# A new written-out order of the steps in five engine programs, with the last two turns apart from the loop

## The chip, the cores and the metric

The kernel runs on one core of a Trainium2 chip. The core has a matrix engine (TensorE, PE in the rows), VectorE (DVE), ScalarE (ACT), GpSimd (POOL), SyncE (SP), which here only issues transfers, and sixteen DMA engines. The metric is the time of one execution on the device, in microseconds, as a median over runs.

## The reference

The input x has 32 batches of 512 tokens with 256 features. Two blocks follow each other, each added to its input.

```python
x = x + attention(layernorm(x), ...)
x = x + ffn(layernorm(x), ...)
```

Attention works within a batch. For each token: a charge q = tanh(x W_charge + b), its powers q^0 to q^4; a normalised projection (shell), whose product with omega plus a bias goes through cosine and sine; the outer product of powers and waves, times W_combine, gives 64 features phi. The logits are phi phi^T, times a factor that decays with the distance of two tokens, over a temperature; a causal softmax of them weighs the values, and W_out closes.

```python
phi = tp @ W_combine.T
logits = jnp.einsum('bnd,bmd->bnm', phi, phi) * T / temp
attn = jax.nn.softmax(jnp.where(causal, logits, -jnp.inf), axis=-1)
out = jnp.einsum('bnm,bmd->bnd', attn, V)
```

The second block holds 64 slots. A hidden layer (gelu) routes each token to its best 8 of 64 slots by a softmax of these 8 (alpha). Each slot gathers the tokens weighted by alpha, a GRU cell makes new slots of that, and each token receives alpha times the new slots' values.

## The kernel before

The 32 batches go through as 16 pairs k = 0..15, with the two batches of a pair as d = 0, 1. A step is a small function that issues the instructions of one piece of work of one pair on one engine, and its name says what: `proj(k, d, t)` on TensorE is the projection of token tile t. `build()` has one program for each engine, and the order of the steps in each is written out by hand, as a list of calls. An engine works strictly in the order of its program; the five meet only through semaphores, on which a step waits for what it reads and for a free buffer. So the order of the lists decides who waits.

Each program has a prologue (the first pairs, written out), a loop `for it in range(3, NP - 1)` of 12 turns, and a tail (the last pair). One turn works on five pairs at once: it projects pair p = it + 2, does the softmax of n = it + 1, the hidden layer and the routing of f = it, the slots of m = it - 1, and the additions to the output of g = it - 2. PSUM's eight banks are dealt out in three rings in the order in which steps take them.

The steps that the text names. TensorE: `first_warm` (L588) and `warm(n)` (L593), matmuls whose result nobody reads; `weights_setup` and `bias_setup` (L311), which multiply the weight matrices together; `xn_t` and other transposes (L317); `proj` (L343); `phi` (L388, L390); `logits` (L409 to L415); `e_t`, the transposes of the softmax (L317); `values` (L438); `hidden` (L466); `route` (L478); `rt_t` (transposes of the routing logits) and `al_t` (of alpha) (L317); `gather` (L500); `gi_t`; `gx_rz` and `gx_n`, the gates (L515); `slot_v` (L559); `out_mm` (L579). VectorE: `ln_stats` (L883), `xn_low` (xl, L889), `vs` (L902), `qk_full` (QK, L961 and L962), `row_max` (L971), `attended` (L979, L983) and its `lm_stats` (L994), `xm_low` (xmL, L1002), `top` and `shift` (the choice of 8 slots), `gathered` (rw, GIN, L1053 to L1059), `slot_values` (SV, L1098), `finish` (L1107), and `end_norm_a`, `end_norm_b` (xm of pair 15, d = 0 and 1, L264). ScalarE: `ln_norm` (xn, L708), `sine` (L742), `z_copy` (Z, L750), `expo` (E, L759), `gelu`, `gi_copy` (GI, L811), `rz_tanh`. A function outside the table that ScalarE has at hand makes it load another one first (ACT_TABLE_LOAD). GpSimd: `square`, `power` (L254), `ln_scale`, `lm_scale` and others.

SyncE issues the loads of x (`load_x`, L1488, one 512 KB batch each), of the weights (`weight_loads`: W_shell, omegaT, W_scT, counted on the semaphore wa; `first_loads`: eleven, from log_temp to the second row of decay; `slot_loads`: seventeen), the moves `z_moves`, which bring the powers of Z to the partitions where phi reads them as xmT (L1503), and the stores (L1512, L1516). x has ten buffers. TensorE's `weights_setup` waits for wa.

The order of SyncE's program before, and TensorE's loop and tail:

```python
load_x(0); weight_loads(); load_x(1); load_x(2); first_loads(); load_x(3); slot_loads()
...
hidden(z, 0); hidden(z, 1)
gx_n(y)
warm(4)
route(z); al_t(y); rt_t(z); out_mm(x, 1)
warm(21)
gather(z); slot_v(y); gi_t(z)
```

(x, y, z are pairs 13, 14, 15.)

Of the kernel before, what the change touches and what calls it, by code (L numbers as in the profile page):

```python
# [88 lines left out]
def build(nc, a, out):  # L89
    ctx = ExitStack()  # L90
    with ctx:
# [204 lines left out]
        def _(e):  # L296
# [333 lines left out]
            first_warm()  # L630
            weights_setup(); xn_t(0, 0, 0); xn_t(0, 0, 1); bias_setup(); xn_t(0, 1, 0); xn_t(0, 1, 1)
            proj(0, 0, 0); proj(0, 0, 1); proj(0, 0, 2); proj(0, 0, 3); xn_t(1, 0, 0); xn_t(1, 0, 1)
            proj(0, 1, 0); proj(0, 1, 1); proj(0, 1, 2); proj(0, 1, 3); slot_setup(); gates_setup()
            xn_t(1, 1, 0); q_t(0); proj(1, 0, 0); proj(1, 0, 1); xn_t(1, 1, 1); proj(1, 0, 2); proj(1, 0, 3)
            proj(1, 1, 0); z_t(0); proj(1, 1, 1); phi(0); proj(1, 1, 2); logits(0, 0); proj(1, 1, 3)
# [5 lines left out]
            values(1, 0); e_t(1, 2); xm_t(0, 0, 0); proj(2, 1, 3); e_t(1, 3); values(1, 1); values(1, 2)
            xm_t(0, 0, 1); values(1, 3); xn_t(3, 0, 1); logits(1, 2); xm_t(0, 1, 0); xm_t(0, 1, 1)
            e_t(1, 4); hidden(0, 0); hidden(0, 1); e_t(1, 5); e_t(1, 6); values(1, 4); q_t(2); route(0)
            xn_t(3, 1, 0); values(1, 5); z_t(2); xn_t(3, 1, 1); rt_t(0); values(1, 6); e_t(1, 7)
            proj(3, 0, 0); values(1, 7); proj(3, 0, 1); proj(3, 0, 2); phi(2); xn_t(4, 0, 0); proj(3, 0, 3)
            proj(3, 1, 0); xm_t(1, 0, 0); logits(2, 0); proj(3, 1, 1); proj(3, 1, 2); e_t(2, 0)
            proj(3, 1, 3); e_t(2, 1); values(2, 0); e_t(2, 2); xm_t(1, 0, 1); logits(2, 1); values(2, 1)
            xm_t(1, 1, 0); xm_t(1, 1, 1); hidden(1, 0); e_t(2, 3); gather(0); logits(2, 2); q_t(3)
            hidden(1, 1); xn_t(4, 0, 1); values(2, 2); gi_t(0); values(2, 3); route(1); e_t(2, 4); gx_rz(0)
            values(2, 4); z_t(3); e_t(2, 5); xn_t(4, 1, 0); gx_n(0); e_t(2, 6); values(2, 5); xn_t(4, 1, 1)  # L650
            values(2, 6); rt_t(1); e_t(2, 7); proj(4, 0, 0); proj(4, 0, 1); phi(3); values(2, 7); slot_v(0)
            logits(3, 0); al_t(0); proj(4, 0, 2); proj(4, 0, 3); proj(4, 1, 0); e_t(3, 0); xm_t(2, 0, 0)
            xm_t(2, 0, 1); proj(4, 1, 1); proj(4, 1, 2); proj(4, 1, 3); e_t(3, 1); e_t(3, 2); values(3, 0)
            values(3, 1); xm_t(2, 1, 0); xm_t(2, 1, 1); e_t(3, 3); logits(3, 1); out_mm(0, 0); values(3, 2)
            q_t(4); hidden(2, 0); hidden(2, 1); values(3, 3); e_t(3, 4); logits(3, 2); out_mm(0, 1)
# [959 lines left out]
```

## Time and profile before

| what | value |
|---|---|
| runs (three) | 725.48, 726.18, 726.43 us; median 726.18 |
| the profiled execution: span, from its first to its last instruction | 729.0 us |
| busy share of TensorE, VectorE, ScalarE, GpSimd | 97%, 85%, 58%, 53% |
| mean granted clock of TensorE | 0.992 |
| chain that ended last: TensorE, VectorE | 85%, 5% |

Times are from the start of the span. The profiled execution is one of its own, longer than the three runs. A timeline row gives the start, the duration, the instruction with tiles out<-in and the count, and in brackets how long the engine had been idle before and what released it. The granted clock is a share of full speed: 1.00 is 2.4 GHz, 0.50 is 1.2 GHz. Ends of matmuls are modelled, so neighbouring rows overlap a little.

### The profile page before, as it was taken

Reading aid. Unit: us, or ns where it says so; the run is one execution under the profiler, and the core shown is the slowest. Engines: PE = TensorE matmul, PEld = TensorE weight load, DVE = VectorE, ACT = ScalarE, POOL = GpSimd, SP = SyncE. Lnnn points to the kernel's source line nnn. Section 1 sums busy time; section 2 is a strip of 40 time slices with the busy share of each in tenths; the row PEclk is TensorE's granted clock in tenths of the full one; section 3 lists DMA queues with packets and bytes.
Section 4 is the critical chain, followed back from the end, with each engine's and each line's share of the span. In section 5 each row is a group of like instructions: output and inputs, shape, how many; then the busy total and the mean of one; then the engine's idle time right before and its main releaser. Section 6 shows DMA issues by size and latency. Waiting matters only on the chain.

```text
span 729.0 us, 15002 instructions
## 1 busy us (share of the span) xinstructions
PE 707.8 (97%) x4592; PEld 558.7 (77%) x4592; DVE 620.3 (85%) x1899; ACT 424.9 (58%) x840; POOL 387.0 (53%) x828
## 2 busy tenths in 40 slices
PE   7998999999999999999999999999999999999896
PEld 4977777777797887778697787879788777867684
DVE  5887888788989898998989899898989899887865
ACT  4539475736456584656648574655757565565441
POOL 4526577363565646476564747556574646653300
...
GB/s 217 112 145 43 45 28 32 29 31 65 111 89 87 6 155 16 116 59 117 58 47 129 3 125 51 116 58 79 98 1 144 31 117 59 59 59 59 1 7 167
DMA packets 49110, 54.12 MB, mean 74 GB/s; under 512 B 6214, under 2 KB 40584, under 8 KB 49032
## 3 DMA queue, kind: packets, MB, share of 16 engines
...
## 4 chain that ended last, share of the span: by engine, by line
PE 85%; DVE 5%; DMA 2%; ACT 2%; POOL 2%; issue 2%; SPq 0%; DVEq 0%; ACTq 0%; POOLq 0%
PE ps L438 17%; PE ps L317 16%; PE ps L343 15%; PE ps L466 6%; PE ps L409 6%; PE ps L515 5%; PE ps L500 4%; PE ps L579 4%; PE ps L388 4%; PE ps L559 2%; PE ps L478 2%; POOL Z L254 2%; PE ps L390 2%; DMA xmT<-Z 1%; DMA X<-in_x 1%
## 5 line engine op out<-in xcount | busy, mean ns | idle before, releaser
L438 PE MATMUL ps<-VS,ET 128*128 128x257 f32 x640 | 159.4, 383 | 0.8 <-ACT ET L769 0.5
L438 PEld LDWEIGHTS ps<-VS,ET 128*128 128x128 f32 x640 | 112.5, 189 | 24.3 <-issue 11.7
L254 POOL TENSOR_TENSOR Z<-Z,QB 128x512 f32<-128x512 f32 x60 | 76.5, 1275 | 98.0 <-ACT Z L750 96.3
L708 ACT ACTIVATE xn<-X,rs 128x256 f32<-128x256 f32 x128 | 66.3, 592 | 73.3 <-POOL rs L1322 73.2
L769 ACT ACTIVATE ET<-ps 128x128 f32<-128x128 f32 (+3 forms) x128 | 55.2, 436 | 69.3 <-PE ps L317 67.9
L343 PE MATMUL ps<-W1h,xh 128*128 128x354 f32 x256 | 88.9, 347 | 0.2 <-DVE xl L889 0.2
L902 DVE TENSOR_TENSOR VS<-ps,biasM 128x354 f32<-128x354 f32 x128 | 66.3, 522 | 24.8 <-PE ps L343 24.7
L759 ACT ACTIVATE E<-ps,nmax 128x128 f32<-128x128 f32 (+3 forms) x128 | 64.3, 525 | 35.7 <-DVE nmax L971 34.2
L343 PE MATMUL ps<-W1l,xh 128*128 128x354 f32 x256 | 84.2, 329 | 0.0
L343 PE MATMUL ps<-W1h,xl 128*128 128x354 f32 x256 | 83.3, 325 | 0.0
L264 POOL TENSOR_SCALAR xm<-X,rs 128x256 f32<-128x256 f32 x120 | 65.8, 562 | 4.7 <-POOL rs L1343 4.7
L983 DVE SCALAR_TENSOR_TENSOR X<-ps,rinv,X 128x256 f32<-128x256 f32 x128 | 61.9, 484 | 4.6
L971 DVE TENSOR_REDUCE nmax<-ps 128x1 f32<-128x128 f32 (+3 forms) x128 | 58.7, 480 | 0.4 <-PE ps L415 0.4
L246 POOL TENSOR_TENSOR tg<-VS 128x256 f32<-128x256 f32 x30 | 18.7, 623 | 75.0 <-DVE VS L902 75.0
L317 PE MATMUL ps<-ident,E 128*128 128x128 f32 x320 | 53.6, 273 | 1.4 <-DVE lg L1030 0.6
L343 PEld LDWEIGHTS ps<-W1h,xh 128*128 128x128 f32 x256 | 49.1, 192 | 5.2 <-issue 4.9
L883 DVE BATCH_NORM_STATS2 stats<-X 128x6 f32<-128x256 f32 x128 | 47.0, 412 | 7.0 <-DMA X<-in_x 7.0
L889 DVE TENSOR_TENSOR xl<-ps,xh 128x512 fp32r<-128x512 f32 x64 | 42.8, 685 | 11.5 <-ACT xh L718 11.4
L409 PE MATMUL ps<-QK 64*128 64x128 f32 (+3 forms) x256 | 50.2, 475 | 0.7 <-ACT E L759 0.5
L718 ACT ACTIVATE xh<-ps 128x512 fp32r<-128x512 f32 x64 | 36.5, 595 | 23.4 <-PE ps L317 19.8
L515 PE MATMUL ps<-GI,wih 128*128 128x128 f32 x384 | 48.3, 276 | 1.3 <-ACT GI L811 1.2
L994 DVE BATCH_NORM_STATS2 stats<-X 128x6 f32<-128x256 f32 x128 | 49.5, 414 | 0.1
...
## 6 DMA issues: line engine op xcount, KB each, us to landing
...
```

Of the source, the lines that this page charges most:

```text
L254: e.tensor_tensor(Z[:, i + 1, :], Z[:, i, :], QB[:, :], ALU.mult).then_inc(s["zm"], 1)
L264: ins = e.tensor_scalar(xm[:, b % 4, t, 0:D], X[:, b % NX, t, :], rs2[:, d, 2, t:t + 1], rs2[:, d, 1, t:t + 1], ALU.add, ALU.mult)
L317: ins = e.transpose(p[0:m, j * 128:j * 128 + 128], block_in, ident[:, :])
L343: ins = e.matmul(p[:, 0:FEATS], x[:, d, c, t * 128:t * 128 + 128], w[:, c, :], start=j == 0, stop=j == 5)
L409: e.matmul(banks[d][:, c:c + w], QK[own(d), 0, rows], QK[own(d), 1, 0:w], start=True, stop=False, skip_group_check=True)
L438: ins = e.matmul(p[:, 0:D + 1], ET[:, r % 2, j * 128:j * 128 + 128], VS[:, (2 * k + d) % 4, j, 0:D + 1], start=j == 0, stop=j == i)
L515: ins = e.matmul(p[:, at_col:at_col + 128], wih[:, c, j * 128:j * 128 + 128], GI[:, k % 2, c, :, :].rearrange("p b s -> p (b s)"), start=c ...
L708: ins = e.activation(xn[:, d, t, :], X[:, b % NX, t, :], ACT.Identity, bias=rs[:, d, 2, t:t + 1], scale=rs[:, d, 1, t:t + 1])
L759: e.activation(E[:, r % 3, 0:w], at["lg", r], ACT.Exp, bias=nmax[:, r % 8:r % 8 + 1]).then_inc(s["E"], 1)
L902: e.tensor_tensor(VS[:, b % 4, t, :], at["vs", b, t][:, 0:FEATS], biasM[:, :], ALU.add).then_inc(s["vs"], 1)
L971: e.tensor_reduce(nmax[:, r % 8:r % 8 + 1], at["lg", r], AX.X, ALU.max, negate=True).then_inc(s["nmax"], 1)
L983: e.scalar_tensor_tensor(X[:, b % NX, i, :], at["av", r][:, 0:D], rinv[:, r % 8:r % 8 + 1], X[:, b % NX, i, :], ALU.mult, ALU.add).then_in ...
```

## The change

The steps and their instructions are the same, apart from a wait that stood in TensorE's tail and now stands in `warm`; their order is another one in each of the five programs. The loop has ten turns instead of twelve, `range(3, 13)`, and turns 13 and 14 and the last pair are written out. `load_x` takes a pair and d, and ScalarE's logarithm of the temperature is now a function, `softplus_log`. The lists are long; the diff shows a part of each that the text speaks of.

```diff
             def warm(n):
+                e.wait_ge(s["E"], 8 * NP)
                 for _ in range(n):
...
-            xn_t(2, 0, 1); e_t(0, 6); values(0, 5); e_t(0, 7); values(0, 6); proj(2, 0, 0); xn_t(2, 1, 0)
-            xn_t(2, 1, 1); proj(2, 0, 1); proj(2, 0, 2); phi(1); xn_t(3, 0, 0); proj(2, 0, 3); logits(1, 0)
+            z_t(1); xn_t(2, 0, 1); values(0, 4); values(0, 5); xn_t(2, 1, 0); e_t(0, 6); proj(2, 0, 0)
+            values(0, 6); proj(2, 0, 1); xn_t(2, 1, 1); phi(1); proj(2, 0, 2); e_t(0, 7); logits(1, 0)
...
-            for it in range(3, NP - 1):
+            for it in range(3, 13):
...
-                values(n, 1); e_t(n, 3); hidden(f, 0); hidden(f, 1); q_t(p); values(n, 2); e_t(n, 4)
+                hidden(f, 0); q_t(p); values(n, 2); e_t(n, 4); hidden(f, 1); logits(n, 2); route(f); e_t(n, 5)
...
+            gather(13); logits(15, 0); out_mm(12, 0); gi_t(13); xm_t(14, 0, 0); e_t(15, 0); gx_rz(13)
...
-            expo(0, 4); probs_t(0, 3); expo(0, 5); probs_t(0, 4); sine(1); expo(0, 6); probs_t(0, 5)
-            z_copy(1); xn_high(2, 0, 1); expo(0, 7); probs_t(0, 6); ln_norm(2, 1); ln_norm(3, 0)
+            probs_t(0, 4); probs_t(0, 5); z_copy(1); xn_high(2, 0, 1); expo(0, 6); xn_high(2, 1, 0)
...
-            lm_stats(z, 6); attended(z, 7); lm_stats(z, 7); slot_values(x); gathered(y); end_norm_a_setup()
-            finish(x, 0, 0); finish(x, 0, 1); xm_low(z, 0, 0); end_norm_b_setup(); xm_low(z, 0, 1); gates(y)
+            lm_stats(15, 6); slot_values(13); attended(15, 7); lm_stats(15, 7); gathered(14)
+            end_norm_a_setup(); finish(13, 0, 0); finish(13, 0, 1); end_norm_b_setup(); xm_low(15, 0, 0)
...
-            rnorm(0); square(1, 0); ln_scale(2, 0); square(1, 1); rnorm(1); ln_scale(2, 1); ln_scale(3, 0)
+            rnorm(0); ln_scale(2, 0); square(1, 0); ln_scale(2, 1); square(1, 1); rnorm(1); power(1, 0)
...
-            load_x(0); weight_loads(); load_x(1); load_x(2); first_loads(); load_x(3); slot_loads()
+            load_x(0, 0); first_loads(); load_x(0, 1); weight_loads(); load_x(1, 0); load_x(1, 1)
```

SyncE's queue from its beginning. Before:

```order
L1488 DMA X<-in_x 128x4x256
L1479 DMA X<-in_W_shell 64x256
L1479 DMA X<-in_omegaT 64x32
L1479 DMA VS<-in_W_scT 128x2x65
L1488 DMA X<-in_x 128x4x256 x2
L1479 DMA X<-in_log_temp 128x1
L1479 DMA X<-in_rff_bias 128x32
L1479 DMA wc<-in_W_combineT 128x2x64
L1479 DMA w<-in_W_combineT 64x64 x2
L1479 DMA wx<-in_W_combineT 64x64 x4
L1479 DMA U<-in_decay 128x512
L1479 DMA Wk<-in_decay 128x512
```

And now:

```order
L1523 DMA X<-in_x 128x4x256
L1514 DMA X<-in_log_temp 128x1
L1514 DMA X<-in_rff_bias 128x32
L1514 DMA wc<-in_W_combineT 128x2x64
L1514 DMA w<-in_W_combineT 64x64 x2
L1514 DMA wx<-in_W_combineT 64x64 x4
L1514 DMA U<-in_decay 128x512
L1514 DMA Wk<-in_decay 128x512
L1523 DMA X<-in_x 128x4x256
L1514 DMA X<-in_W_shell 64x256
L1514 DMA X<-in_omegaT 64x32
L1514 DMA VS<-in_W_scT 128x2x65
```

The three weight loads W_shell, omegaT and W_scT moved from the second place to behind the eleven first loads and the second batch of x.

VectorE in the loop, around qk_full, whose two products with U and Wk are the rows QK; L979 and L983 are attended, L994 its statistics. Before:

```order
L883 BN_STATS stats<-X 128x6 x2
L979 RECIPROCAL rinv<-ps 128x1
L983 SCALAR_TENSOR_TENSOR X<-ps,rinv,X 128x256
L883 BN_STATS stats<-X 128x6 x2
L994 BN_STATS stats<-X 128x6 x4
L961 TENSOR_TENSOR QK<-ps,U 128x512
L962 TENSOR_TENSOR QK<-ps,Wk 128x512
L883 BN_STATS stats<-X 128x6 x2
L979 RECIPROCAL rinv<-ps 128x1
L983 SCALAR_TENSOR_TENSOR X<-ps,rinv,X 128x256
L1053 TENSOR_SCALAR rw<-ps 128x1
```

And now (the same steps have later line numbers: 992 and 996, 1007, 974 and 975):

```order
L1007 BN_STATS stats<-X 128x6
L896 BN_STATS stats<-X 128x6 x2
L1007 BN_STATS stats<-X 128x6
L992 RECIPROCAL rinv<-ps 128x1
L996 SCALAR_TENSOR_TENSOR X<-ps,rinv,X 128x256
L1007 BN_STATS stats<-X 128x6 x2
L974 TENSOR_TENSOR QK<-ps,U 128x512
L975 TENSOR_TENSOR QK<-ps,Wk 128x512
L896 BN_STATS stats<-X 128x6 x2
L1066 TENSOR_SCALAR rw<-ps 128x1
L1068 RECIPROCAL rw<-rw 128x1
L1072 TENSOR_SCALAR GIN<-ps,rw 128x256
```

A second attended, that of the pair's last block, and its statistics moved from behind the two rows of QK to ahead of them.

TensorE in the tail, from the last products of hidden(15, 1) on; L593 (now L594) is warm, L478 route, L579 out_mm, L500 gather. Before:

```order
L466 MATMUL ps<-xmL,w1h 128x512
L466 MATMUL ps<-xmT,w1l 128x512
L515 MATMUL ps<-GI,wih 128x128 x4
L593 MATMUL ps<-ident 128x128 x4
L478 MATMUL ps<-hT,w 64x512 x2
L317 MATMUL ps<-ident,AL 128x128 x4
L317 MATMUL ps<-ident,hT 128x128 x4
L579 MATMUL ps<-SV,aT 128x256 x4
L593 MATMUL ps<-ident 128x128 x21
L500 MATMUL ps<-xm,AL 64x257 x8
L559 MATMUL ps<-Wvo,SN 128x256 x2
```

And now:

```order
L466 MATMUL ps<-xmL,w1h 128x512
L466 MATMUL ps<-xmT,w1l 128x512
L515 MATMUL ps<-GI,wih 128x128 x4
L478 MATMUL ps<-hT,w 64x512 x2
L594 MATMUL ps<-ident 128x128 x3
L317 MATMUL ps<-ident,hT 128x128 x4
L594 MATMUL ps<-ident 128x128 x4
L579 MATMUL ps<-SV,aT 128x256 x4
L594 MATMUL ps<-ident 128x128 x21
L500 MATMUL ps<-xm,AL 64x257 x8
```

The warming matmuls ahead of route are gone, and so are the transposes of AL between route and those of hT; three steps of warm stand behind route instead, four behind the transposes of hT, and twenty-one ahead of gather as before.

## Rows read from the trace of the kernel before

**Rows 1.** Part 1 of the page: busy time and share of the span.

```profile
PE 707.8 (97%) x4592; PEld 558.7 (77%) x4592; DVE 620.3 (85%) x1899; ACT 424.9 (58%) x840; POOL 387.0 (53%) x828
```

**Rows 2.** Busy time by stretch: from:to, its length, busy us (count) by engine, clock, DMA share, GB/s.

```profile
0.00:20.00 20.00, 15.53 (x53) 9.36 (x54) 11.58 (x43) 9.10 (x18) 9.22 (x37) 0.95 0.76 234
20.00:47.00 27.00, 26.40 (x148) 24.78 (x147) 22.12 (x67) 11.78 (x19) 9.66 (x30) 0.85 0.45 141
47.00:194.00 147.00, 142.11 (x892) 108.31 (x893) 124.19 (x374) 89.46 (x175) 85.67 (x166) 1.00 0.20 49
277.70:319.50 41.80, 41.80 (x280) 33.40 (x278) 37.48 (x116) 25.97 (x52) 24.32 (x52) 1.00 0.28 77
```

**Rows 3.** Timeline of SyncE's queue at the start: start, duration in us, instruction.

```profile
0.72 0.44 SPq L1488 DMA_DIRECT2D X<-in_x  x1
...
2.45 0.59 SPq L1479 DMA_DIRECT2D VS<-in_W_scT  x1
...
4.14 0.81 SPq L1479 DMA_DIRECT2D X<-in_log_temp  x1
...
11.91 0.43 SPq L1479 DMA_DIRECT2D Wk<-in_decay  x1
```

**Rows 4.** DMA issues of the first 30 us: issue, KB, median us to landing.

```profile
VS<-in_W_scT SPq DMA_DIRECT2D x1, 65.0 KB, 6.9
X<-in_W_shell SPq DMA_DIRECT2D x1, 64.0 KB, 4.5
```

**Rows 5.** Timeline of TensorE at the start; in brackets idle before and its releaser.

```profile
9.52 2.83 PE L311 MATMUL ps<-X 128*128 128x256 f32 x12 [1.24 <-DMA VS<-in_W_scT]
...
16.77 0.66 PE L317 MATMUL ps<-ident,xn 128*128 128x128 f32 x4 [1.02 <-ACT xn L708]
18.20 1.12 PE L317 MATMUL ps<-ident,xn 128*128 128x128 f32 x4 [0.77 <-DVE xl L889]
```

**Rows 6.** Waits of TensorE from 47 to 194 us (total, times, longest); timelines of ScalarE, GpSimd.

```profile
PE ps L388 <- DMA xmT<-Z: 1.9, 3, 0.7
...
64.97 1.28 ACT L759 ACT_TABLE_LOAD   x1
...
67.90 5.36 POOL L254 TENSOR_TENSOR Z<-Z,QB 128x512 f32<-128x512 f32 x4 [1.81 <-ACT Z L750]
```

**Rows 7.** Timelines of VectorE and TensorE in a steady turn, around qk_full.

```profile
279.26 0.69 DVE L961 TENSOR_TENSOR QK<-ps,U 128x512 f32<-128x512 f32 x1 [0.54 <-PE ps L390]
279.87 0.68 DVE L962 TENSOR_TENSOR QK<-ps,Wk 128x512 f32<-128x512 f32 x1
...
280.88 0.49 PE L409 MATMUL ps<-QK 64*128 64x128 f32 x4
```

**Rows 8.** Timeline of TensorE in the tail.

```profile
659.89 2.02 PE L515 MATMUL ps<-GI,wih 128*128 128x128 f32 x16 [0.57 <-ACT GI L811]
...
686.20 1.96 PE L500 MATMUL ps<-xm,AL 128*64 128x257 f32 x16 [1.56 <-DVE SV L1098]
...
702.23 0.63 PE L317 MATMUL ps<-ident,hT 128*128 128x128 f32 x4 [0.29 <-ACT hT L795]
...
703.85 4.96 PE L593 MATMUL ps<-ident 128*128 128x128 f32 x42
709.12 1.96 PE L500 MATMUL ps<-xm,AL 128*64 128x257 f32 x16 [0.32 <-DVE AL L283]
```

**Rows 9.** Timeline of VectorE in the tail.

```profile
684.68 0.17 DVE L979 RECIPROCAL rinv<-ps 128x1 f32<-128x1 f32 x1 [0.39 <-PE ps L438]
684.88 0.48 DVE L983 SCALAR_TENSOR_TENSOR X<-ps,rinv,X 128x256 f32<-128x256 f32 x1
685.40 0.43 DVE L994 BATCH_NORM_STATS2 stats<-X 128x6 f32<-128x256 f32 x1
685.74 0.41 DVE L1098 TENSOR_TENSOR SV<-ps,bSV 128x256 f32<-128x256 f32 x1
...
692.42 1.37 DVE L264 TENSOR_SCALAR xm<-X,rs 128x256 f32<-128x256 f32 x4
```

More of the change, by code:

```diff
@@ L628, in gates_setup @@
                           "slot_mm", "slot_evac", 2)
[L630 to L635, printed above, removed]
@@ L641, in _ @@
[L641 to L645, printed above, removed]
@@ L646, in _ @@
[L646 to L655, printed above, removed]
@@ L669, in _ @@
-            x, y, z = NP - 3, NP - 2, NP - 1
-            xm_t(z, 0, 0); xm_t(z, 0, 1); gx_rz(y); xm_t(z, 1, 0); xm_t(z, 1, 1)
-            e.wait_ge(s["E"], 8 * NP)
-            warm(3)
-            hidden(z, 0); hidden(z, 1)
-            gx_n(y)
-            warm(4)
-            route(z); al_t(y); rt_t(z); out_mm(x, 1)
-            warm(21)
-            gather(z); slot_v(y); gi_t(z)
-            warm(2)
-            gx_rz(z)
-            out_mm(y, 0); gx_n(z); out_mm(y, 1); al_t(z); slot_v(z); out_mm(z, 0); out_mm(z, 1)
+            first_warm(); weights_setup(); xn_t(0, 0, 0); xn_t(0, 0, 1); bias_setup(); xn_t(0, 1, 0)
@@ new lines, in _ @@
+            e_t(2, 1); xm_t(1, 0, 1); values(2, 0); xm_t(1, 1, 0); e_t(2, 2); logits(2, 1); values(2, 1)
+            hidden(1, 0); xm_t(1, 1, 1); e_t(2, 3); q_t(3); logits(2, 2); gather(0); values(2, 2)
+            hidden(1, 1); e_t(2, 4); gi_t(0); xn_t(4, 0, 1); values(2, 3); route(1); xn_t(4, 1, 0)
+            values(2, 4); e_t(2, 5); z_t(3); gx_rz(0); gx_n(0); e_t(2, 6); values(2, 5); e_t(2, 7); rt_t(1)
+            values(2, 6); proj(4, 0, 0); xn_t(4, 1, 1); proj(4, 0, 1); phi(3); values(2, 7); logits(3, 0)
@@ new lines, in _ @@
+            slot_v(0); proj(4, 0, 2); xm_t(2, 0, 0); proj(4, 0, 3); e_t(3, 0); proj(4, 1, 0); al_t(0)
+            proj(4, 1, 1); xm_t(2, 0, 1); proj(4, 1, 2); proj(4, 1, 3); e_t(3, 1); xm_t(2, 1, 0); values(3, 0)
+            e_t(3, 2); values(3, 1); xm_t(2, 1, 1); logits(3, 1); out_mm(0, 0); q_t(4); e_t(3, 3)
+            values(3, 2); hidden(2, 0); e_t(3, 4); hidden(2, 1); values(3, 3); logits(3, 2); out_mm(0, 1)
+            gather(1); route(2); z_t(4); gi_t(1); rt_t(2); values(3, 4); e_t(3, 5); gx_rz(1); al_t(1); gx_n(1)
@@ new lines, in _ @@
+            route(13); logits(14, 2); e_t(14, 5); values(14, 3); rt_t(13); z_t(15); values(14, 4)
+            values(14, 5); slot_v(12); e_t(14, 6); al_t(12); e_t(14, 7); values(14, 6); values(14, 7); phi(15)
+            gather(13); logits(15, 0); out_mm(12, 0); gi_t(13); xm_t(14, 0, 0); e_t(15, 0); gx_rz(13)
+            e_t(15, 1); values(15, 0); gx_n(13); xm_t(14, 0, 1); e_t(15, 2); logits(15, 1); out_mm(12, 1)
+            xm_t(14, 1, 0); values(15, 1); e_t(15, 3); xm_t(14, 1, 1); hidden(14, 0); logits(15, 2)
@@ new lines, in _ @@
+            hidden(14, 1); values(15, 2); e_t(15, 4); route(14); values(15, 3); e_t(15, 5); rt_t(14); al_t(13)
+            values(15, 4); e_t(15, 6); values(15, 5); slot_v(13); e_t(15, 7); values(15, 6); values(15, 7)
+            gather(14); out_mm(13, 0); gi_t(14); xm_t(15, 0, 0); xm_t(15, 0, 1); gx_rz(14); xm_t(15, 1, 0)
+            xm_t(15, 1, 1); hidden(15, 0); al_t(14); hidden(15, 1); gx_n(14); route(15); warm(3); rt_t(15)
+            warm(4); out_mm(13, 1); warm(21); gather(15); slot_v(14); gi_t(15); gx_rz(15); out_mm(14, 0)
@@ L683, in _ @@
+            gx_n(15); out_mm(14, 1); al_t(15); slot_v(15); out_mm(15, 0); out_mm(15, 1); warm(2)
         @block.scalar
@@ L1306, in _ @@
+            slot_values(15); finish(15, 0, 0); finish(15, 0, 1); finish(15, 1, 0); finish(15, 1, 1)
         @block.gpsimd
```

322 lines of the change are left out of this document (184 added, 138 removed).

## The prediction

> **What bounds the kernel.** I read the views from coarse to fine. The page's first part gives TensorE 97% of the span [rows 1]: any gain has to come out of the missing 3%. The table by stretches says where those are [rows 2]. In a steady turn TensorE is busy for all 41.80 us of 41.80, so no order of the same steps can win anything there; it can only lose. In the fill, from 47 to 194 us, it is busy for 142.11 of 147.00 us, so 4.9 us are idle. Before 47 us it starts late and runs for a while at half clock, and after 653 us it waits for single results. So I priced the start, the fill, the steady turns and the tail apart. The start I read from SyncE's queue [rows 3], the landing times [rows 4] and TensorE's first instructions [rows 5]; the fill from the waits [rows 6]; the steady turn at its tightest hand-over [rows 7]; the tail from TensorE [rows 8] and VectorE [rows 9].
>
> All durations are from the profiled execution, whose span is 729.0 us, 2.8 us (0.4%) over the median of the runs, 726.18 us. I take differences from it and put them on the median.
>
> **Start: a loss of 4.6 us.** TensorE's first real work, weights_setup, waits for the load of W_scT [rows 5]: that load is issued third, at 2.45 us [rows 3], and TensorE starts at 9.52. In the new order eleven other loads (log_temp to Wk) and one more batch of x go ahead of the three weight loads. In the trace those eleven take SyncE from 4.14 us to the end of Wk's issue at 12.34, 8.2 us [rows 3]. If they take as long when they come first, x's issue ends at about 1.2 us, the eleven at 9.4, x(0,1) at 9.9, and W_scT is issued at 11.1. If each costs the 0.6 us of most single issues, the eleven take 6.6 and W_scT is issued at 9.5. It then needs between 4.5 us (as W_shell) and 6.9 us (as itself) to land [rows 4]. The weights are thus there between 14.0 and 18.0 us; I take the middle, 15.9, as nothing speaks for an end. TensorE starts 6.4 us later. Not all of it lasts: a little later TensorE waited 1.02 us for xn and 0.77 us for xl [rows 5], results of x alone or of the weights' copies on VectorE; both are likely to be ready under a later start, so 1.8 us come back. 6.4 - 1.8 = 4.6 us, with 2.7 and 6.7 as the ends. From there on TensorE is on the path to the end, so the loss goes through whole.
>
> The stretch from 20 to 47 us had a mean granted clock of 0.85 [rows 2]: time at the level of 1.2 GHz between stretches at 2.4 GHz, in all 0.15 times 27, 4 us lost, in two spells, 2 us each. I leave that loss as it is: TensorE begins with the same six warming matmuls and then waits for the weights in either order. The Trainium skill, page "TensorE: Matmul & The Clock Gate", section "HAM oscillation — how this bites in real kernels", says that an engine that waits for a DMA between bursts falls back to the low clock and begins the next burst cold. By that rule the longer wait for the weights would bring a third spell, and the sum would be 2 us worse. In the trace the wait for the weights was 1.24 us [rows 5] and the mean clock of the first 20 us 0.95 [rows 2], so it bears out neither a spell at that wait nor its absence at a longer one.
>
> **Fill: a gain of 3.0 us.** 4.9 us are idle there [rows 2], of which the three waits of phi for xmT make 1.9 [rows 6]. They end a chain over four engines: ScalarE's sine, a reload of the exponential's table of 1.28 us at 64.97, Z's copy, four powers on GpSimd, 5.36 us, the move. In the new order the copy of Z(1) stands before the expo that reloads the table, GpSimd's square(1,1) follows earlier work, and steps that wait are pushed behind steps that are ready. But for the first phi less independent TensorE work stands ahead of it (proj(2,0,2) now follows phi), so there the earlier Z mostly meets an earlier need. I count the 1.9 us of these waits as to be had half, and the other 3.0 us of smaller waits by two thirds: 0.95 + 2.0 = 3.0 us. Bounds: all 4.9 us, and a loss of 1 us, two more waits of 0.5 us, shorter than phi's longest, 0.7.
>
> **Steady turns: 0.** All ten turns keep the same work, and TensorE has no idle time to give [rows 2]. Hand-overs with slack stay covered: xn_t moved between two proj, hidden(f,1) moved behind e_t(n,4). The bound above nothing is a wait of 0.5 us in each turn, 5 us; below, nothing.
>
> **Tail: a gain of 3.3 us.** (1) gx_rz(13) waited 0.57 us for GI [rows 8]; now xm_t(14,0,0) and e_t(15,0) stand before it: -0.6. (2) Gather(14) waited 1.56 us, for slot_values(13), SV [rows 8], which VectorE began only at 685.74, behind attended(15,7) and its statistics, begun at 684.68 [rows 9]. Put ahead of these, it is 1.1 us earlier, and what follows too. xm(15,1), at 692.42, stood behind a first xmL; it now stands before it, 1.1 us more: -2.2 for the last transposes. (3) warm(3) and warm(4), seven steps of 0.236 us (21 took 4.96 [rows 8]), 1.65 us, leave the place ahead of route, but al_t(14), four transposes as rt_t's, some 0.5 us, comes in ahead: -1.15. So rt_t(15), at 702.23, would start 0.6 + 2.2 + 1.15 = 4.0 us earlier. (4) From there to gather(15), at 709.12, it was 6.9 us, and gather waited 0.32 us for AL, VectorE's choice of the eight slots [rows 8]. TensorE now has more to do between the two, as warm(4) comes in: rt_t and out_mm 1.62, warm(4) 0.95, warm(21) 4.96, in all 7.5 us. So 0.6 to 0.7 us go back: 3.3 us. Ends: 1.5 us, if items (1) and (3) are all; 5 us, if the waits behind 709 us shrink too. Two warm matmuls at the very end run beside VectorE's last addition and the store, and cost nothing; if these were not there they would cost 0.5 us.
>
> SyncE's other moves (x loaded a batch earlier, the first moves of Z behind it) cost nothing: SyncE has idle time, and the buffers of x are five pairs deep.
>
> **Sum.** +4.6 - 3.0 + 0 - 3.3 = -1.7 us, on the median 724.5 us.
>
> **Rivals.**
> (A) The weights come early and the fill gains in full. For it: SyncE's issues are long only where many come at once. Start +2.7, fill -4.9, tail -3.3: -5.5, 720.7 us. Against it: W_scT still stands behind eleven loads and a batch of x on one queue, and its own landing was the longer of the two [rows 4].
> (B) Slower: a new wait in each steady turn. Its place is qk_full. In the trace VectorE idles 0.54 us before it and ends it at about 280.55, and logits starts at 280.88 [rows 7], 0.3 us later. The new order puts attended(f,7) and its statistics ahead of qk_full: 0.17 + 0.48 + 0.43 = 1.08 us, as the same step took in the tail [rows 9]. 0.54 go into the idle time, 0.3 into the slack, 0.2 would be left as a wait of TensorE; if what is ahead is also late, up to 0.5. Ten turns make 2 to 5 us: 726.5 to 729.5 us, 728.5 as its number. It decides from 0.32 us a turn on, where it outweighs 1.7 us by the measurable bound. For it: no row shows reserve there. Against it: VectorE is busy for 37.48 of 41.80 us [rows 2], and work before qk_full can run ahead.
> (C) The start and the rest cancel: the weights land at 17 us (+5.7), the fill gives 2, the tail 3: about 726.9 us, no change.
> (D) The third spell at the low clock, by the mechanism that TensorE idles from 8.3 us until the weights come and then runs setup and proj at the half rate: 2 us on the sum, 726.5 us. The page of the clock named above states this rule.
>
> **How the numbers follow.** A measurement of this kernel can tell about 0.2%, 1.45 us, from no change: faster is below 724.7, slower above 727.6. My sum lies just beyond the first bound, so much of its chance spills over. Forecast, 724.5 with 2 us around it: 0.37. (A) 0.20. (B) 0.20. (C) 0.13. (D) 0.10. Faster: half of the forecast's, 0.20, nearly all of (A), 0.20, and some 0.04 of the rest, 0.44. Slower: 0.05 of the forecast, 0.16 of (B), 0.06 of (C), 0.04 of (D), 0.31. The same: 0.25. The range runs from 718.5 us, (A) with the tail at its end of 5 us, to 730.0 us, (B) with 0.5 us a turn and a little more; about 2 in 10 lie outside. The forecast's own range is 722.5 to 726.5.
>
> **What would show it.** Start: TensorE's setup behind first_warm at about 16 us, waiting for W_scT, and the last xn_t ahead of proj at 22.8 instead of 18.20. Fill: three waits of phi for xmT together under 1.2 us, and a busy time over 144 us in the 147 us from phi(0) on. Steady: turns of 41.8 us with no wait; a wait of logits for QK would be (B). Tail: gather(14) without a wait for SV, and from the last phi to the end 3 us less. Wrong it is if weights_setup starts under 13 us or over 19, or if a steady turn differs by over 0.2 us.

## The result and the profile after

The changed kernel is slower: 738.21 us (median of four, 735.05 to 742.94) against 726.30 us (725.48 to 726.57), a ratio of 1.0170 with an interval of 1.0129 to 1.0212. The prediction was 724.5 us with a range to 730.0. The profiled execution is the slowest of the four, 742.94 us, with a span of 741.1 us. Its mean granted clock is 0.983; the others had 0.986, 0.993 and 0.995, in the order of their times.

TensorE's share is still 97%, with 7.6 us more busy time for the same instructions (compare [rows 1]); this is the first part of the page of the kernel after:

```profile
PE 715.4 (97%) x4592; PEld 563.3 (76%) x4592; DVE 625.8 (84%) x1899; ACT 420.8 (57%) x840; POOL 388.4 (52%) x828
```

The starts of phi cut both executions at nearly the same steps. The chain that ended last, of the kernel before (start, duration, what), with phi of pairs 4, 14 and 15:

```profile
192.97 1.87 PE ps L388 x8
...
610.67 1.87 PE ps L388 x8
...
652.44 1.87 PE ps L388 x8
```

The same of the kernel after:

```profile
202.83 1.94 PE ps L388 x8
...
624.65 1.87 PE ps L388 x8
...
667.71 1.87 PE ps L388 x8
```

phi of pair 0 (L381) in TensorE's timelines, before:

```profile
47.24 0.64 PE L381 MATMUL ps<-Z,wc 64*64 64x512 f32 x1
```

And after:

```profile
57.60 0.64 PE L381 MATMUL ps<-Z,wc 64*64 64x512 f32 x1
```

So the difference of the spans, 12.1 us, falls into: to phi(0) +10.4; the fill from phi(0) to phi(4) 145.23 instead of 145.73, -0.5; ten turns to phi(14) 421.82 instead of 417.70, +4.1; turn 13 (it = 13), the first of the two written out, which ends with phi(15), 43.06 instead of 41.77, +1.3; from phi(15) to the end, with turn 14 and the last pair, 73.39 instead of 76.56, -3.2. One piece of work changed sides: the new list has proj(1,1,2), six matmuls of some 1.0 us in all, ahead of phi(0), the old one behind it. With the same work on either side it is +9.4 to phi(0) and +0.5 in the fill.

**Start.** SyncE's queue after (start, duration in us; compare [rows 3]):

```profile
1.22 0.49 SPq L1514 DMA_DIRECT2D X<-in_log_temp  x1
...
7.16 0.43 SPq L1514 DMA_DIRECT2D Wk<-in_decay  x1
...
9.30 0.59 SPq L1514 DMA_DIRECT2D VS<-in_W_scT  x1
```

W_scT is issued at 9.30 us instead of 2.45. TensorE's timeline (with idle time before and its releaser; compare [rows 5]):

```profile
14.98 5.17 PE L311 MATMUL ps<-X 128*128 128x256 f32 x12 [5.82 <-DMA VS<-in_W_scT]
...
21.98 4.40 PE L311 MATMUL ps<-X 1*128 1x65 f32 x10
...
27.93 0.64 PE L343 MATMUL ps<-W1h,xh 128*128 128x354 f32 x1
```

The weights land at 14.98 us, and TensorE has waited 5.82 us. But setup then takes 5.17 us instead of 2.83 and the bias 4.40 instead of 2.45: the busy time by stretch (columns as in [rows 2]) shows why.

```profile
10.00:15.00 5.00, 0.02 (x1) 0.05 (x1) 0.96 (x3) 1.63 (x4) 0.00 (x0) 0.79 1.07 292
15.00:20.00 5.00, 5.00 (x12) 3.27 (x12) 4.12 (x20) 2.08 (x4) 2.86 (x8) 0.50 1.08 370
20.00:25.00 5.00, 5.00 (x16) 3.66 (x17) 2.78 (x6) 1.20 (x2) 3.75 (x19) 0.50 0.68 200
25.00:30.00 5.00, 5.00 (x19) 4.29 (x19) 1.97 (x4) 2.28 (x5) 0.49 (x2) 0.50 0.00 0
```

From 15 to 30 us the granted clock is 0.50, the level of 1.2 GHz, throughout this execution, the slowest of the four. The first proj comes at 27.93 instead of 18.97.

**Steady turns.** The timeline of TensorE of the kernel after in one turn (L466 is hidden, L317 with QN is q_t):

```profile
312.82 0.39 PE L466 MATMUL ps<-xmL,w1h 128*128 128x512 f32 x1
313.05 0.39 PE L466 MATMUL ps<-xmT,w1l 128*128 128x512 f32 x1
313.65 0.63 PE L317 MATMUL ps<-ident,QN 128*128 128x128 f32 x4 [0.21 <-ACT QN L728]
```

And of ScalarE in the same turn (L825 is n_tanh, L782 xm_copy, L761 expo, L728 charge, which writes QN):

```profile
310.86 0.68 ACT L825 ACTIVATE gn<-gn,bihn 128x128 f32<-128x128 f32 x2
311.44 1.07 ACT L782 ACTIVATE xmT<-ps 128x512 fp32r<-128x512 f32 x2
312.40 0.59 ACT L761 ACTIVATE E<-ps,nmax 128x384 f32<-128x384 f32 x1
312.86 0.64 ACT L728 ACTIVATE QN<-VS 128x512 f32<-128x512 f32 x1
```

TensorE's next step after hidden(f,0) is q_t. It waits for QN, the last 0.21 us of it shown as idle time: from the start of hidden's sixth matmul to q_t 0.60 us go by, where neighbouring matmuls follow in 0.23. The hand-over at qk_full, where rival (B) looked for a wait, shows none. The waits of TensorE (total, times, longest) after the fill, from 205 to 622 us:

```profile
PE ps L317 <- ACT QN L728: 2.0, 10, 0.2
```

Ten waits, one a turn, and no other line. The same view of the fill, from 57 to 205 us:

```profile
PE ps L388 <- DMA xmT<-Z: 1.9, 2, 1.4
PE ps L317 <- ACT E L761: 1.7, 1, 1.7
PE ps L559 <- DVE SN L1103: 1.7, 1, 1.7
```

e_t (E) and slot_v (SN) wait 1.7 us each, and phi as long in all as before [rows 6].

**Tail.** TensorE's timeline after, the rows that answer to [rows 8]. gather(14), the first, had waited 1.56 us for SV:

```profile
699.24 1.96 PE L500 MATMUL ps<-xm,AL 128*64 128x257 f32 x16
...
713.65 0.63 PE L317 MATMUL ps<-ident,hT 128*128 128x128 f32 x4
...
716.16 4.96 PE L594 MATMUL ps<-ident 128*128 128x128 f32 x42
721.05 1.96 PE L500 MATMUL ps<-xm,AL 128*64 128x257 f32 x16
```

None of these steps waits now.

### The profile page after: what moved, and what is told of

Same layout as the page of the kernel before. It is cut to its first block, busy times and chain, and to the rows that moved or that the text cites. A ratio compares the mean times of both kernels' runs of the same rounds, so it can differ in the third digit from the quotient of the medians.

```text
span 741.1 us, 15002 instructions
## 1 busy us (share of the span) xinstructions
PE 715.4 (97%) x4592; PEld 563.3 (76%) x4592; DVE 625.8 (84%) x1899; ACT 420.8 (57%) x840; POOL 388.4 (52%) x828
## 4 chain that ended last, share of the span: by engine, by line
PE 84%; DVE 5%; DMA 3%; ACT 2%; issue 2%; SPq 2%; POOL 2%; DVEq 0%; ACTq 0%; POOLq 0%
PE ps L317 16%; PE ps L438 16%; PE ps L343 16%; PE ps L409 6%; PE ps L515 5%; PE ps L579 4%; PE ps L466 4%; PE ps L388 4%; PE ps L500 3%; PE ps L478 2%; PE ps L390 2%; PE ps L559 2%; PE ps L311 1%; DMA out_x<-X 1%; ACT E L761 1%
## 5 line engine op out<-in xcount | busy, mean ns | idle before, releaser
L254 POOL TENSOR_TENSOR Z<-Z,QB 128x512 f32<-128x512 f32 x60 | 78.3, 1305 | 91.6 <-ACT Z L752 89.9
L343 PE MATMUL ps<-W1h,xh 128*128 128x354 f32 x256 | 90.7, 354 | 0.4 <-DVE xl L902 0.4
L761 ACT ACTIVATE E<-ps,nmax 128x128 f32<-128x128 f32 (+3 forms) x128 | 65.6, 531 | 22.4 <-DVE nmax L984 20.9
L915 DVE TENSOR_TENSOR VS<-ps,biasM 128x354 f32<-128x354 f32 x128 | 64.5, 519 | 10.7 <-PE ps L343 9.0
L264 POOL TENSOR_SCALAR xm<-X,rs 128x256 f32<-128x256 f32 x120 | 67.9, 580 | 2.9 <-POOL rs L1375 2.8
L317 PE MATMUL ps<-ident,E 128*128 128x128 f32 x320 | 55.0, 276 | 2.0 <-ACT E L761 1.7
L896 DVE BATCH_NORM_STATS2 stats<-X 128x6 f32<-128x256 f32 x128 | 46.8, 412 | 10.3 <-DMA X<-in_x 10.3
L317 PEld LDWEIGHTS ps<-ident,E 128*128 128x128 f32 x320 | 39.2, 141 | 18.0 <-issue 10.0
L782 ACT ACTIVATE xmT<-ps 128x512 fp32r<-128x512 f32 x64 | 35.6, 594 | 29.8 <-PE ps L317 29.7
L1007 DVE BATCH_NORM_STATS2 stats<-X 128x6 f32<-128x256 f32 x128 | 51.6, 415 | 0.5
```

Source lines behind the costliest of these rows:

```text
L254: e.tensor_tensor(Z[:, i + 1, :], Z[:, i, :], QB[:, :], ALU.mult).then_inc(s["zm"], 1)
L264: ins = e.tensor_scalar(xm[:, b % 4, t, 0:D], X[:, b % NX, t, :], rs2[:, d, 2, t:t + 1], rs2[:, d, 1, t:t + 1], ALU.add, ALU.mult)
L317: ins = e.transpose(p[0:m, j * 128:j * 128 + 128], block_in, ident[:, :])
L343: ins = e.matmul(p[:, 0:FEATS], x[:, d, c, t * 128:t * 128 + 128], w[:, c, :], start=j == 0, stop=j == 5)
L761: e.activation(E[:, r % 3, 0:w], at["lg", r], ACT.Exp, bias=nmax[:, r % 8:r % 8 + 1]).then_inc(s["E"], 1)
L915: e.tensor_tensor(VS[:, b % 4, t, :], at["vs", b, t][:, 0:FEATS], biasM[:, :], ALU.add).then_inc(s["vs"], 1)
```

## The experiments

Each was compared with runs of the kernel before on the same chip. "Turn" is the mean distance of two phi from phi(4) to phi(14), in kernels named a_ from phi(5) to phi(14), in the profiled execution.

| kernel | time, us (median) | before beside it | ratio, interval | turn, us |
|---|---|---|---|---|
| a_weights | 730.83 | 726.46 | 1.0059 (1.0043 to 1.0075) | 42.26 |
| b_late | 734.50 | 726.46 | 1.0110 (1.0082 to 1.0138) | 41.75 |
| a_hidden | 741.56 | 726.46 | 1.0225 (1.0176 to 1.0273) | 42.57 |
| a_warm | 736.48 | 726.46 | 1.0137 (1.0115 to 1.0158) | 42.14 |
| a_charge | 730.55 | 726.09 | 1.0063 (1.0042 to 1.0084) | 42.18 |
| b_tail | 723.75 | 726.09 | 0.9963 (0.9948 to 0.9977) | 41.77 |
| b_body | 731.23 | 726.09 | 1.0073 (1.0050 to 1.0096) | 42.19 |
| mix | 725.73 | 726.09 | 0.9995 (0.9985 to 1.0005) | 41.78 |
| body_old_act | 744.14, one run | 726.13 | | 43.33 |
| body_old_dve | 734.03, one run | 726.13 | | 42.44 |
| body_only_pe | 745.03, one run | 726.13 | | 43.55 |
| late_warm | 730.36 | 726.13 | 1.0053 (1.0036 to 1.0070) | 41.75 |
| mix_phi | 727.40 | 726.58 | 1.0013 (0.9996 to 1.0031) | 41.75 |
| b_tail5 | 723.69 | 726.58 | 0.9951 (0.9934 to 0.9968) | 41.75 |

### The transfers of the start, undone and alone

a_weights, in the kernel after:

```diff
-            load_x(0, 0); first_loads(); load_x(0, 1); weight_loads(); load_x(1, 0); load_x(1, 1)
+            load_x(0, 0); weight_loads(); load_x(0, 1); load_x(1, 0); first_loads(); load_x(1, 1)
```

> The changed kernel with the transfers of the start in the order of before (weight_loads second, first_loads behind x(1,0)); nothing else undone. Theory: the late weights cost TensorE 5.5 us at weights_setup and, by the longer wait, a stretch at the half clock up to 30 us. Then weights_setup starts near 9.5 us again, proj near 19 us, phi(0) near 47 to 49 us instead of 57.6, and the time falls by 7 to 10 us, to about 729 us. Rival: the new order of the prologue on the engines costs as much as the transfers; then phi(0) stays at 52 us or later and the time falls by less than 5 us.

It took 7.4 us less than the kernel after. TensorE's timeline of its start:

```profile
9.18 2.76 PE L311 MATMUL ps<-X 128*128 128x256 f32 x12
...
17.31 0.40 PE L343 MATMUL ps<-W1h,xh 128*128 128x354 f32 x1
```

b_late, in the kernel before:

```diff
-            load_x(0); weight_loads(); load_x(1); load_x(2); first_loads(); load_x(3); slot_loads()
+            load_x(0); first_loads(); load_x(1); weight_loads(); load_x(2); load_x(3); slot_loads()
```

> The kernel before with the transfers of the start in the new order alone. Theory: 7 to 10 us slower than before, with the weights at about 15 us and a low clock from there to about 30 us. Rival, that only the new prologue together with the late weights is slow: under 4 us slower, as VectorE and ScalarE have other things ready.

It is 8.0 us slower than before. The order of three loads is thus worth 7.4 to 8.0 us, with the old programs of the other engines as with the new; the rivals fell. Two details missed. In a_weights phi(0) came at 44.86 us, earlier than the 47 to 49 given. And in b_late the low clock did not last to 30 us. TensorE's timeline of its start:

```profile
14.81 4.94 PE L311 MATMUL ps<-X 128*128 128x256 f32 x12 [5.87 <-DMA VS<-in_W_scT]
...
23.93 0.41 PE L343 MATMUL ps<-W1h,xh 128*128 128x354 f32 x1
```

Setup is slow, 4.94 us, but the clock is 0.57 from 15 to 20 us and 1.00 again from 20 to 25.

### Idle time and low clock in the start

a_warm and late_warm keep TensorE busy until the weights land, in the kernel after and in b_late. In both:

```diff
-                for _ in range(6):
+                for _ in range(13):
                     e.matmul(banks[2][:, :], E[:, 0, 0:128], E[:, 0, :], start=True, stop=True)
```

> The changed kernel with thirteen instead of six matmuls in first_warm, whose result nobody reads, so that TensorE is busy until the weights land. Theory that the wait brings the low clock: the granted clock stays at 1.00 from 15 to 25 us, weights_setup takes about 2.9 instead of 5.2 us, the step to proj is 5 us shorter, and the time falls by 4 to 6 us if the last warming matmul ends by 15 us. Rival, that the low clock comes from the sparse work behind the wait: it shows again at 15 to 25 us and the time stays within 2 us.

> The kernel before with the start's transfers in the new order and thirteen instead of six matmuls in first_warm, so that TensorE does not idle until the weights come. It parts the cost of the late weights, 8.0 us with six matmuls, into idle time and low clock. Theory: the weights come 5.5 us later, TensorE keeps 1.00 of its clock, phi(0) comes at 48.3 us (42.8 at full clock before, plus 5.5), and the kernel is 5 to 6 us slower than before; the other 2 to 3 us were low clock. Rival: later waits swallow 1.8 us, as predicted, and it is 3.5 to 4 us slower.

The clock stayed at full level behind the warming matmuls. Busy time by stretch, a_warm:

```profile
15.00:20.00 5.00, 5.00 (x26) 3.61 (x26) 4.64 (x23) 2.13 (x5) 2.90 (x8) 1.00 1.08 371
20.00:25.00 5.00, 5.00 (x31) 4.41 (x31) 4.97 (x12) 4.15 (x9) 3.75 (x19) 1.00 0.65 185
```

TensorE's timeline of late_warm:

```profile
1.44 14.45 PE L588 MATMUL ps<-E 128*128 128x512 f32 x26 [1.44 <-DVE E L1110]
15.72 2.76 PE L311 MATMUL ps<-X 128*128 128x256 f32 x12
...
22.66 0.41 PE L343 MATMUL ps<-W1h,xh 128*128 128x354 f32 x1
```

Setup takes 2.76 us again, 2.2 less than in b_late. late_warm is 4.2 us slower than before, between the 5 to 6 of its theory and the 3.5 to 4 of its rival; b_late, without the warming, 8.0. By these medians 4.2 of the 8 us are idle time (in late_warm setup began at 15.72, right behind the last warming matmul, so up to 0.9 of it may be the warming's own) and 3.8 low clock. In the new programs the same split is another one: a_warm is 5.7 us over a_weights, and it gained 1.7 us on the kernel after, less than the 4 to 6 expected. So the 7.4 to 8.0 us are shown, and the split is an estimate: the interval of b_late alone is 4 us wide, and low clock falls elsewhere too.

In the profiled a_warm the clock is 0.91 and 0.74 from 55 to 65 us, behind the wait for E that mix shows below; its four runs spread from 734.96 to 738.60 with mean clocks of 0.997 to 0.992. In the profiled b_late and late_warm it falls near 695 us, in the tail, which takes 78.2 us instead of 76.6; whether that comes of the loads no row shows.

### The loop's body

b_body puts the new body of four engines into the kernel before:

```diff
             for it in range(3, NP - 1):
                 p, n, f, m, g = it + 2, it + 1, it, it - 1, it - 2
-                xn_t(p, 0, 0); xn_t(p, 0, 1); gx_rz(m); e_t(n, 0); proj(p, 0, 0); proj(p, 0, 1)
+                xn_t(p, 0, 0); xn_t(p, 0, 1); gx_rz(m); e_t(n, 0); proj(p, 0, 0); proj(p, 0, 1); xn_t(p, 1, 0)
...
```

> The kernel before with the new order of the loop's body in TensorE, ScalarE, VectorE and GpSimd, in all twelve turns. Theory: the body loses 0.38 us in each turn by itself; 4 to 5.5 us slower, about 731 us, and turns of 42.15 us. Rival, that the body only loses where it follows the late start or the new prologue: turns of 41.8 us and no difference over 1 us.

Turns of 42.19 us, 5.1 us slower in twelve turns: the body loses 0.42 us a turn by itself. Two attempts to take the wait for QN away, on TensorE (a_hidden) and on ScalarE (a_charge, with the early weights):

```diff
-                hidden(f, 0); q_t(p); values(n, 2); e_t(n, 4); hidden(f, 1); logits(n, 2); route(f); e_t(n, 5)
+                hidden(f, 0); hidden(f, 1); q_t(p); values(n, 2); e_t(n, 4); logits(n, 2); route(f); e_t(n, 5)
...
-                xm_copy(f, 1, 0); xm_copy(f, 1, 1); expo(n, 4); charge(p); probs_t(n, 3); expo(n, 5)
+                xm_copy(f, 1, 0); xm_copy(f, 1, 1); charge(p); expo(n, 4); probs_t(n, 3); expo(n, 5)
```

> The changed kernel with hidden(f,1) put back ahead of q_t in the loop, on TensorE alone. Theory: q_t came 1.4 us earlier in the turn and waits for QN, which stalls TensorE 0.36 us in each of ten turns; undone, a turn takes 41.8 instead of 42.15 us and the time falls by 3 to 4 us. Rival: the wait moves on to z_t, which ends the same chain of ScalarE's copy and sine; then the turn stays over 42.0 us and the time within 1.5 us.

> The changed kernel with the start's transfers as before and, in ScalarE's loop, charge(p), which writes QN, put back ahead of expo(n,4). Theory: TensorE's wait of q_t for QN is ScalarE's order: n_tanh, 0.58 us, and expo(n,4), 0.46 us, stand ahead of charge now. With expo(n,4) behind it QN is ready 0.46 us earlier, more than the 0.36 us that TensorE lost; a turn takes 41.8 instead of 42.2 us, and the time falls by 3 to 4 us against the kernel with the early weights, to about 727 us. Rival: the wait goes over to xmL, as it did when hidden(f,1) was put back; then the turn stays at 42.1 us or more and the time within 1.5 us of 730.8.

Both theories failed, and the rivals were right that the wait moves on, though not where to. The waits of TensorE in a_hidden, over the whole span:

```profile
PE ps L466 <- DVE xmL L1015: 4.6, 10, 0.5
```

and in a_charge:

```profile
PE ps L478 <- ACT hT L792: 1.9, 10, 0.2
```

The wait for QN is gone in both, and another stands in its place ten times: for xmL from VectorE, 0.46 us, or for hT from ScalarE, 0.19 us. a_hidden's turn grew to 42.57 us, 0.4 over that of the kernel after, and its time by 3.4 us, more than the 1.5 its rival allowed; a_charge stayed at 42.18 us and 730.55. So the wait for QN is only the first of several hand-overs without slack. Then I took single engines' lists out of the new body, or put one in alone. body_old_act and body_old_dve are b_body with the old list on ScalarE or on VectorE, body_only_pe is the kernel before with the new list on TensorE.

> The kernel before with the new body in TensorE, VectorE and GpSimd, ScalarE's body as before. Theory that ScalarE's new order (n_tanh and expo(n,4) ahead of charge, probs later) makes the turn long: turns fall from 42.15 to 41.8 us. Rival, that VectorE brings its results later and ScalarE only passes this on: turns stay at 42.1 us or more, with a wait for hT or xmL in place of that for QN.

> The same with VectorE's body as before and the other three new. Theory of ScalarE: turns stay at 42.1 us with the wait for QN. Rival, VectorE: attended(n,1), 0.65 us, and row_max(n,5), 0.55 us, now stand ahead of xm_low(f,1); undone, turns of 41.8 us.

> The kernel before with the new body on TensorE alone. If TensorE's split of hidden with q_t between is enough by itself, turns are 42.1 us or more with a wait for QN. If ScalarE or VectorE has to be late too, turns are 41.8 us: before, charge ended at 301.85 us and q_t's new place, 1.4 us ahead of 303.6, is 302.2, so I expect 41.8 us and no wait for QN.

No turn came back to 41.8 us, the figure of body_old_act's theory, of body_old_dve's rival and of the expectation of body_only_pe. Each of the three is one run. The waits of TensorE from 190 to 600 us in body_only_pe:

```profile
PE ps L317 <- ACT xn L707: 14.8, 10, 1.5
```

In body_old_act:

```profile
PE ps L317 <- ACT xn L707: 8.8, 10, 0.9
```

And in body_old_dve:

```profile
PE ps L343 <- DVE X L1106: 2.2, 9, 0.2
PE ps L317 <- ACT QN L725: 1.9, 10, 0.2
```

TensorE's new list alone makes turns of 43.55 us: it asks for xn_t(p,1,0) and xn_t(p,1,1) between two proj, and the old ScalarE has xn only 1.5 us later. ScalarE's new list, with ln_norm(p,1) early, is the answer to that: without it, in body_old_act, TensorE waits 0.9 us for xn in each turn. With VectorE's old list the wait for QN stays, as the theory said, but one for VectorE's finish (L1106) comes in, and the turn is 42.44 us instead of 42.1. The lists are made for each other, and together they still leave 0.4 us. Which set of moves would give 41.8 us isn't shown, and GpSimd's new list was not run by itself.

### The last pair, the prologue, and the two together

b_tail is the kernel before with the tail of the last pair as after. On VectorE, and likewise on TensorE and ScalarE:

```diff
-            lm_stats(z, 6); attended(z, 7); lm_stats(z, 7); slot_values(x); gathered(y); end_norm_a_setup()
+            lm_stats(z, 6); slot_values(x); attended(z, 7); lm_stats(z, 7); gathered(y)
...
```

> The kernel before with the new order of the last pair on TensorE, ScalarE and VectorE alone. Theory: from phi(15) to the end 73.5 instead of 76.6 us, as in the changed kernel; 3 us faster, about 723.4 us. Rival: a part of these 3 us came from turn 14, which is written out in the changed kernel; then under 1.5 us.

723.75 us, 2.3 us under the kernel before. From phi(15), at 647.32, to the end of its span, 721.5, it takes 74.2 us; the kernel after takes 73.4, so 0.8 us belong to the order of turn 14: gather(14) stands 33.8 us behind phi(15) before, 32.3 in b_tail and 31.5 in the kernel after. The rival was right that a part came from turn 14, and its "under 1.5 us" was too low.

mix adds the new prologue of TensorE, VectorE, ScalarE and GpSimd, with the transfers as before.

> The new prologue of the four engines and the new order of the last pair, with the start's transfers and the loop of before, twelve turns. Theory, by the sum of the parts: prologue -2.5 us (phi(4) at about 190.3 instead of 193.0), tail -3 us; about 721 us, faster than both kernels. Rival: what the prologue gains is only low clock that the profiled run of before happened to have; then about 723.4 us, as with the new tail alone.

The theory missed, and the rival by less: 725.73 us, no gain on the kernel before, and 2.0 us behind b_tail, where the rival had them equal. The profiled b_tail had a mean clock of 1.00. Busy time by stretch, mix:

```profile
50.00:55.00 5.00, 3.03 (x24) 2.33 (x24) 3.97 (x13) 3.77 (x8) 3.49 (x5) 0.80 0.00 2
55.00:60.00 5.00, 5.00 (x27) 3.10 (x28) 3.37 (x10) 4.56 (x12) 0.00 (x0) 0.86 0.00 0
```

The clock is 0.80 and 0.86. TensorE's timeline of mix shows what was ahead of that:

```profile
53.17 0.45 PE L317 MATMUL ps<-ident,E 128*128 128x128 f32 x1 [1.72 <-ACT E L751]
53.41 1.06 PE L317 MATMUL ps<-ident,QN 128*128 128x128 f32 x4
```

After the wait of 1.72 us for E the four transposes of q_t take 1.06 us; at [rows 8] four transposes of rt_t take 0.63. mix_phi tries to fill that wait:

```diff
-            proj(1, 0, 3); proj(1, 1, 0); proj(1, 1, 1); z_t(0); proj(1, 1, 2); phi(0); proj(1, 1, 3)
-            logits(0, 0); e_t(0, 0); q_t(1); e_t(0, 1); e_t(0, 2); logits(0, 1); e_t(0, 3); values(0, 0)
+            proj(1, 0, 3); proj(1, 1, 0); proj(1, 1, 1); z_t(0); phi(0); proj(1, 1, 2); logits(0, 0)
+            proj(1, 1, 3); e_t(0, 0); q_t(1); e_t(0, 1); e_t(0, 2); logits(0, 1); e_t(0, 3); values(0, 0)
...
-            power_b_setup(); power_c_setup(); ln_stats(2, 1, 1); power_d_setup(); norm_sum(1, 0); vs(1, 1, 2)
-            qk_full(0); vs(1, 1, 3); ln_stats(3, 0, 0); row_max(0, 0); row_max(0, 1); norm_sum(1, 1)
+            power_b_setup(); power_c_setup(); ln_stats(2, 1, 1); power_d_setup(); norm_sum(1, 0); qk_full(0)
+            vs(1, 1, 2); vs(1, 1, 3); ln_stats(3, 0, 0); row_max(0, 0); row_max(0, 1); norm_sum(1, 1)
```

> The mix (new prologue, early weights, loop of before, new last pair) with phi(0) put back ahead of proj(1,1,2) on TensorE, so that one proj stands on either side of logits(0,0) as before, and qk_full(0) ahead of vs(1,1,2) on VectorE. Theory: the mix lost its gain to a low clock from 53 to 58 us that follows TensorE's wait of 1.72 us for E at e_t(0,0), with nothing left to do between logits and e_t; with a proj there that wait falls to 0.5 to 0.9 us, the clock from 50 to 60 us stays at 1.00, and the time falls from 725.7 to 722.5 to 723.5 us, at or under the kernel with the new last pair alone. Rival: the low clock comes anywhere in the thin first 60 us, by chance; then the time stays within 1 us of 725.7.

> The kernel before with the new last pair alone, once more beside the other: 723.75 us again, within 0.5 us, at full clock.

b_tail5 held, at 723.69 us. mix_phi missed, at 727.40 us, also the 1 us that its rival allowed. TensorE's timeline of mix_phi:

```profile
58.13 0.30 PE L317 MATMUL ps<-ident,E 128*128 128x128 f32 x1 [2.81 <-ACT E L751]
```

And its busy time by stretch behind that:

```profile
60.00:65.00 5.00, 5.00 (x19) 3.54 (x20) 3.32 (x10) 3.48 (x8) 0.00 (x0) 0.50 0.00 0
```

The wait for E did not shrink, it became 2.81 us, and low clock followed it again, 0.50 from 60 to 65 us. Its twelve runs go from 725.94 to 731.89 us, with mean clocks from 0.998 to 0.991; b_tail5's seven from 723.01 to 724.58, at 0.997 to 1.000. The other profiled executions fit: of the seven kernels with the new prologue six lose clock between phi(0) and phi(4), from within 2 us of the end of that wait for E on (0.73 from 55 to 60 us in a_weights, 0.66 from 60 to 65 in a_hidden, 0.71 from 55 to 60 in a_charge), and the kernel after alone does not. Of the nine with the old prologue, whose wait at e_t(0,0) is 0.5 us in the kernel before, none does. So there the new prologue is open to low clock and the old one isn't; as no run took the wait away, its part as the cause is argued, not shown. b_tail is the fastest kernel here, twice: 0.9963 and 0.9951 of the kernel before.

## Why the prediction was wrong

The forecast was 1.7 us faster, and it became 11.9 slower. Term by term (the sum stands below) the turns missed by 5.4 us, the fill by 5.0, the start by 3.4 and the tail by 0.1.

**Start, +4.6 predicted: the step that failed is "I leave that loss as it is".** The idle time was about right. The weights came at 14.98 us, between the 14.0 and 18.0 given; setup began 5.5 us later than before, and some of it came back: from setup to the first proj it took 9.45 us before and 6.94 in late_warm, which is 4.2 us slower than before. What I left out was the clock. In all the late loads cost 8.0 us in b_late; by the medians 1.7 to 3.8 us of this are low clock, in the profiled b_late 2.2 us at setup, and in the profiled run of the kernel after far more, 15 us at 0.50. It was there as rival (D), with a chance of 0.10 and a price of 2 us, one spell as those before. The rule was named beside it, the Trainium skill's page "TensorE: Matmul & The Clock Gate", section "HAM oscillation — how this bites in real kernels", that TensorE, after a wait for a DMA, begins its next burst at the low clock. By that rule the start is worse than the idle time alone, and the trace agrees: a wait of 5.82 us, then 0.50; with the wait filled, in a_warm, 1.00. The price of a spell was misread too. The busy time by stretch, before:

```profile
20.00:25.00 5.00, 5.00 (x31) 4.98 (x31) 3.89 (x10) 2.65 (x5) 3.46 (x14) 0.86 0.85 261
...
35.00:40.00 5.00, 5.00 (x25) 5.00 (x24) 3.16 (x11) 1.09 (x2) 0.00 (x0) 0.51 0.06 15
40.00:45.00 5.00, 4.81 (x26) 4.53 (x26) 4.07 (x10) 2.36 (x4) 0.00 (x0) 0.81 1.03 341
```

The 4 us lost there are not "two spells, 2 us each": 0.14 of 5 us is 0.7, and 0.49 and 0.19 of 5 us are 3.4 us behind 35 us. One spell could cost more than 2 us, and the kernel before had low clock in its start without late weights.

**Fill, -3.0 predicted: the step that failed is counting two thirds of the idle time as to be had,** without following the new lists to their own waits. phi still waits 1.9 us for xmT in all, 1.4 of it now in one wait; what the new order saves in small waits it gives back at e_t(0,0), 1.7 us for E, and at slot_v(0), 1.7 us for SN. In mix phi(4) starts at 189.1 us, in b_tail at 187.8; the 0.80 and 0.86 of mix's clock make 1.7 us, so at full clock the new prologue would gain 0.4 us, an estimate from these rows. By the medians mix is 2.0 us behind b_tail, which has the old prologue.

**Steady turns, 0 predicted: +4.1.** "It can only lose" was right, and "hand-overs with slack stay covered" was the step that failed: I had named hidden(f,1) moved behind e_t(n,4) as covered. q_t moved up by the 1.4 us of that half, and charge moved back on ScalarE behind n_tanh and expo(n,4). With either move undone the turn stayed over 42.1 us, at a wait for xmL or hT: the slack was gone at several hand-overs, not at one. Rival (B) had a new wait in each turn, with 0.2 to 0.5 us for its price, and 0.42 was measured; its place, qk_full, was wrong, so that its number came out is luck. The prediction's own sign of being wrong, a turn off by over 0.2 us, came true. Turn 13, written out, lost 1.3 us that I had not priced. TensorE's waits there (total, times, longest), from 622 to 669 us:

```profile
PE ps L438 <- DVE X L996: 0.9, 1, 0.9
```

This wait of the last values for VectorE's X is 0.9 us of it; what the rest is stays open.

**Tail, -3.3 predicted: right, in the main by its own steps.** From phi(15) on, rt_t(15) comes 3.85 us earlier (45.94 instead of 49.79; 4.0 predicted), gather(15) 3.3 (53.34 instead of 56.68), and the end 3.2. The wait for SV is gone, and 0.5 us went back between rt_t and gather, as the warming matmuls now set that distance, 7.40 us (7.5 predicted). The parts of the 3.85 us were off by half a microsecond in opposite ways, which is luck: 2.2 us come before gather(14), where 1.7 were predicted, and 1.6 behind it, for 2.25.

**Sum.** The late loads 8.0 (b_late), the fill 2.0 (mix against b_tail), 4.1 + 1.3 in the turns, -3.2 in the tail: 8.0 + 2.0 + 5.4 - 3.2 = 12.2 us, against 11.9 measured. That it comes so close is partly luck, as medians with wide intervals and single profiled executions are added here. A shorter sum agrees: a_weights, which has all of the change but the late loads, is 4.4 us slower than before, and 4.4 + 8.0 = 12.4. The times of the four runs follow their clocks, 7.9 us for 0.012; drawn out to a clock of 1.00 that makes some 731.8 us, an estimate. Then about half of the 11.9 us is order and idle time (4.2 + 5.4 - 3.2 - 0.4 = 6.0 by the terms above) and half low clock. The profiled run has more clock loss before phi(0) and less fill loss than these medians.
